# Wider product columns in the two middle token stages of an adaLN-FFN kernel, and lows moved between VectorE and GpSimd

## The reference

```python
lora_delta = lora_B @ lora_A * 0.5
wg = (weight + lora_delta).reshape(O, 16, 128)          # groups of 128 inputs
normalized = wg / exp(scale_log)
quantized = cb[searchsorted((cb[:-1] + cb[1:]) / 2, normalized)]   # 32 levels
w_eff = (quantized * scale) + lora_delta
y = x @ w_eff.T                                          # "cond"
result = y @ W_base.T + b_base                           # "ffn"
ax, probs = y @ A_w.T, softmax(y @ router_w.T)
mixed = sum over 8 experts of probs[e] * (ax @ cores[e])
out = x + result + mixed @ B_w.T * 2
```

## Time and profile before

| | |
|---|---|
| median of 3 runs | 2316.75 us (2315.3 to 2317.07) |
| profiled execution, own time | 2317.91 us |
| its span, first to last instruction | 2316.1 us |
| mean granted TensorE clock | 0.993 |
| busy: TensorE, VectorE, ACT, GpSimd | 2240.4, 1969.0, 1496.5, 1381.3 us |

### The profile page before, as it was taken

How to read it: one execution, slowest core, us unless ns; L and a number is a source line. 1 busy time by engine, 2 the same in 40 slices (tenths; PEclk the granted TensorE clock), 3 DMA queues, 4 the chain that set the end, 5 groups by cost and what they waited for, 6 DMA issues and landing times.

```text
span 2316.1 us, 31908 instructions
## 1 busy us (share of the span) xinstructions
PE 2240.4 (97%) x11610; PEld 2022.0 (87%) x11610; DVE 1969.0 (85%) x2509; ACT 1496.5 (65%) x1962; POOL 1381.3 (60%) x894
## 2 busy tenths in 40 slices
PE   3889899999999999999999999999999999999999
PEld 2445479999999989899999989899999999999998
DVE  8999998889997977999997988999996766777776
ACT  7999978989886765666664865666663664122121
POOL 6888846669874534888775635887872132333231
PEclk9999999999999999999999999999999999999999
DMA  5787855444434434666664334666656666646554
GB/s 208 261 287 274 313 211 178 163 147 156 149 129 141 116 109 177 234 239 248 246 229 156 116 105 173 226 247 253 248 211 201 186 189 186 240 190 229 194 218 155
DMA packets 133234, 459.63 MB, mean 198 GB/s; under 512 B 14114, under 2 KB 66914, under 8 KB 96354
## 3 DMA queue, kind: packets, MB, share of 16 engines
q1 hardware_dynamic: 133076, 457.59, 56.7%
HBM read 306.41 MB, written 151.13 MB: 198 GB/s over the span
## 4 chain that ended last, share of the span: by engine, by line
PE 85%; DVE 9%; ACT 3%; DMA 1%; issue 1%; POOL 0%; DVEq 0%; SPq 0%; POOLq 0%; ACTq 0%
PE m L1239 6%; PE m L1238 6%; PE m L1240 6%; DVE acc L1713 6%; PE m L1190 5%; PE m L1192 5%; PE m L1191 5%; PE m L1296 4%; PE m L1298 4%; PE m L1297 4%; PE m L1346 4%; PE m L1348 4%; PE m L1347 4%; PE m L1131 4%; PE m L1307 3%; PE m L1306 3%
## 5 line engine op out<-in xcount | busy, mean ns | idle before, releaser
L1713 DVE SCALAR_TENSOR_TENSOR acc<-mk,dj,acc 128x1024 f32<-128x1024 uint8 x736 | 943.2, 1282 | 66.3 <-ACT mk L1461 47.9
L1461 ACT ACTIVATE mk<-wr,bj 128x1024 uint8<-128x1024 f32 x736 | 811.7, 1140 | 3.0 <-DVE acc L1713 2.1
L2034 POOL TENSOR_TENSOR pp<-pp,tm 128x1024 f32<-128x1024 f32 x184 | 454.0, 2468 | 22.3 <-POOL tm L2020 0.6
L2020 POOL TENSOR_SCALAR tm<-mp,dj 128x1024 f32<-128x1024 uint8 x192 | 226.0, 1178 | 211.0 <-ACT mp L1467 203.5
L1817 DVE TENSOR_TENSOR kl<-kw,kh 128x416 fp32r<-128x416 f32 (+3 forms) x310 | 237.6, 775 | 85.8 <-ACT kh L1496 84.7
L1496 ACT ACTIVATE kh<-kw 128x416 fp32r<-128x416 f32 (+3 forms) x310 | 169.1, 548 | 182.1 <-DMA kw<-in_wb 91.8
L1239 PE MATMUL m<-gl,xh 128*128 128x384 f32 (+2 forms) x800 | 280.9, 351 | 0.0
L1238 PE MATMUL m<-gh,xh 128*128 128x384 f32 (+2 forms) x800 | 280.6, 351 | 0.0
L1240 PE MATMUL m<-gh,xl 128*128 128x384 f32 (+2 forms) x800 | 279.8, 350 | 0.0
L1467 ACT ACTIVATE mp<-wr,bj 128x1024 uint8<-128x1024 f32 x224 | 255.1, 1139 | 0.0
L1773 DVE TENSOR_TENSOR part<-m,part 128x512 f32<-128x512 f32 (+4 forms) x362 | 217.6, 610 | 30.9 <-PE m L1240 16.6
(11 more groups left out here) (249 smaller groups left out, 5169.8 us busy)
## 6 DMA issues: line engine op xcount, KB each, us to landing
part<-part SPq DMA_DIRECT2D x191, 1036.0 KB, 4.8
rows<-in_wb SPq DMA_DIRECT2D x61, 1036.0 KB, 4.8
out<-part SPq DMA_DIRECT2D x31, 1024.0 KB, 4.8
kw<-in_ws SPq DMA_DIRECT2D x128, 208.0 KB, 2.7
xw<-in_x SPq DMA_DIRECT2D x96, 256.0 KB, 3.3
kw<-in_wb SPq DMA_DIRECT2D x92, 192.0 KB, 2.4
wr<-in_w SPq DMA_DIRECT2D x32, 512.0 KB, 5.9
dl<-delta SPq DMA_DIRECT2D x30, 512.0 KB, 5.3
```

Source lines behind the costliest of these rows:

```text
L1461: e.activation(R.mk[m % NM], w, ACT.Identity, bias=R.bj[:, j:j + 1], scale=GROW).then_inc(S["mk"], 1)
L1713: e.scalar_tensor_tensor(R.acc, R.mk[m % NM], R.dj[:, j:j + 1], R.acc, ALU.mult, ALU.add).then_inc(S["ac"], 1)
L2034: e.tensor_tensor(R.pp, first, R.tm[scaled_level(q, i)], ALU.add).then_inc(S["pp"], 1)
```

## The change

Seven things change together.

1. `SW` becomes 680. A product's 680 columns are two matmuls of 340 in neighbouring banks (one PSUM tensor `mm` of five banks; a chain takes banks 0 and 1 or 2 and 3, and the chains change places from pair to pair). Rests become two pieces of 356 columns for each tile, in bank 4 and `pd`. The sums of G's blocks are 1360 wide; the fourth one doesn't fit in the wh buffers any more and lies over a quarter of G that only pair 0 reads, so it is built at pair 1.
2. Pair 15 is mixed as well; pair 1 and pair 15 have their own order of units.
3. `token_sums_low` moves from VectorE to GpSimd; the low part of a pair's second tile (`second_low`) moves from GpSimd to VectorE.
4. In W stages 1 and 2 the low part of each fourth slot (s % 4 == 3) is GpSimd's.
5. W stages 1 and 2 take three halves of levels instead of two and a half, token stages 1 and 2 five instead of five and a half; 14 units at the start and 9 at the end have no levels.
6. At the start of W stages 2 and 3 slots 2 to 5 lie in guest buffers (stage 2: x0, x1, x2 and a token sums buffer).
7. The high and low splits of the next stage's first weights take other places: highs of the last pair at units 3, 7 and 9, GpSimd's lows at 4 and 7, and in stage 1 VectorE's four lows (17, 19, 21, 23) at slots 0 to 3 of W stage 2. The tile store and the fetch of raw half 24 (`half_done`) come after the last unit that adds to the pair's first tile, in pair 15 at unit 9 of 11.

The diff, cut to its core:

```diff
-UNTIL_TOKENS, UNTIL_WEIGHTS = (16, 24, 32), (0, 18.5, 26.5, 32)
+UNTIL_TOKENS, UNTIL_WEIGHTS = (16, 24, 32), (0, 19, 27, 32)
-GUEST = {4: 2, 5: 0}
-GUEST_LAST = {2: 0, 3: 1, 10: 0, 11: 1}
+GUEST = {1: {4: "x2", 5: "x0"}, 2: {2: "x0", 3: "x1", 4: "x2", 5: "sums"},
+         3: {2: "g0", 3: "g1", 4: "x2", 5: "x0", 10: "g0", 11: "g1"}}
-SW = 512
-REST = (HX - SW) // 3 * 2
-MIX = (("prod", 1), ("prod", 2), ("rest", 0, 0), ("rest", 0, 1), ("prod", 6), ("prod", 5), ("rest", 0, 2), ("prod", 7),
-       ("prod", 3), ("rest", 1, 0), ("prod", 4), ("rest", 1, 1), ("rest", 1, 2))
+SW = 680
+SPLIT_SW, REST = 340, HX - SW
+CHAIN_AT = (512 - SPLIT_SW, 3 * 512 - SPLIT_SW)
+MIX = (("prod", 1), ("prod", 2), ("rest", 0, 0), ("prod", 6), ("prod", 5), ("rest", 0, 1), ("prod", 7), ("prod", 3),
+       ("rest", 1, 0), ("prod", 4), ("rest", 1, 1))
+MIX_START = (("prod", 1), ("prod", 2), ("rest", 0, 0), ("rest", 0, 1), ("prod", 6), ("prod", 5), ("rest", 1, 0), ("prod", 7),
+             ("prod", 3), ("rest", 1, 1), ("prod", 4))
+MIX_END = (("prod", 1), ("rest", 0, 0), ("prod", 5), ("prod", 6), ("rest", 0, 1), ("prod", 3), ("prod", 7), ("rest", 1, 0),
+           ("prod", 2), ("prod", 4), ("rest", 1, 1))
-MIX_FIRST, MIX_LAST = 1, PAIRS - 2
+MIX_FIRST, MIX_LAST = 1, PAIRS - 1
-SPREAD_AT, SPREAD_HIGH_AT = (0, 1, 3), (1, 2, 3, 4)
-SPREAD_LOW, SPREAD_LOW_AT = (2, 0, 1, 3), ((0, 4), (0, 5), (0, 6), (1, 2))
+SPREAD_AT, SPREAD_HIGH_AT = ((0, 0), (0, 2), (1, 0)), ((0, 1), (0, 3), (0, 4), (1, 1))
+SPREAD_LOW, SPREAD_LOW_AT = (0, 1, 2, 3), ((0, 5), (0, 6), (1, 1), (1, 5))
+HIGH_SPLIT_AT = {1: {3: (16, 20), 7: (18, 22, 17), 9: (19, 21, 23)}, 2: {3: (24,), 7: (26, 25, 27)}}
+LOW_SPLIT_AT = {1: {4: (16, 20), 7: (18, 22)}, 2: {4: (24,), 7: (26,), 9: (25,), 10: (27,)}}
+LOW_SPLIT_LATER = {2: (17, 19, 21, 23), 3: ()}
-WAIT_LEVELS, END_LEVELS, WAIT_SLOTS = 8, 11, 4
+WAIT_LEVELS, END_LEVELS, WAIT_SLOTS = 14, 9, 4
...
+def weight_by_pool(g, s):
+    return g < LAST and s % 4 == 3
+def unit_chain(u):
+    return (u[0] + (u[2] in (2, 3, 5))) % 2
+def low_by_vector(g, t):
+    return g in MIXED and mixed(t // 2) and t % 2 == 1
...
# mixed_tokens_of
-            if at == (11 if mixed(p) else 9) and mixed(p + 1):
+            if at == (MIX_OF[p].index(("prod", 3)) + 2 if mixed(p) else 9):
                 yield ("token_sums_high", g, p + 1)
-                if p:
-                    yield ("token_sums_low", g, p + 1)
-            if (p, at) == (1, 1):
-                yield ("token_sums_low", g, 1)
-            if (p, at) == (1, 5):
+                yield ("token_sums_low", g, p + 1)
+            if (p, at) == (0, 8):
                 yield ("late_normalised", g)
-        if at == (9 if mixed(p) else 5):
+        if p == PAIRS - 1 and at == 5:
+            yield ("next_weights", g)
+        if at == half_done_at(p):
             yield ("half_done", g, p)
-        if p == PAIRS - 1 and at == 6:
-            yield ("next_weights", g)
...
# tensor_program.mul
+            n, first = at[0], CHAIN_AT[unit_chain(UNITS_OF[g][k])]
+            pieces = ((0, SPLIT_SW), (SPLIT_SW, SW))
+                for c0, c1 in pieces:
+                    e.matmul(R.mm[:, first + c0:first + c1], high, oh[:, c0:c1], start=kp == 0 and n in (1, 2, 5), stop=False,
+                             skip_group_check=n in (3, 4, 6, 7))
+                # the same for (high, ol) and (low, oh)
...
# vector_program
+    def second_low(g, t):
+        xw, xl, xh = R.token(g, t)
+        e.wait_ge(S["xh"], NT * g + t + 1)
+        e.wait_ge(S["qs"], 4 * sums_count(g, t // 2))
+        e.tensor_tensor(xl, xw, xh.bitcast(F32), ALU.subtract).then_inc(S["xd"], 1)
...
# gpsimd_program
+    def weight(g, s):
+        w = slot_width(g, s)
+        e.wait_ge(S["gh"], NS * (g - 1) + s + 1)
+        kw, kl, kh = R.ring(g, s)
+        e.tensor_tensor(kl[:, 0:w], kw[:, 0:w], kh[:, 0:w].bitcast(F32), ALU.subtract).then_inc(S["pl"], 1)
```

More of the change, by code:

```diff
@@ L524, in first_at_home @@
 def first_at_home(g, s):
-    guests = {**GUEST, **(GUEST_LAST if g == LAST else {})}
-    return s not in guests and all(k in guests for k in range(s % RING, s, RING))
+    return s not in GUEST[g] and all(k in GUEST[g] for k in range(s % RING, s, RING))
 def wait_consumed(e, S, q):
@@ L537, in wait_consumed, with weight_lows, wait_weight @@
         e.wait_ge(S["used"], NS * g)
+def weight_by_pool(g, s):
+    return g < LAST and s % 4 == 3
+def weight_lows(g, s, pool):
+    return sum(1 for i in range(1, g + 1) for u in range(slots_of(i)) if (i, u) <= (g, s) and weight_by_pool(i, u) == pool)
+def wait_weight(e, S, g, s):
+    if weight_by_pool(g, s):
+        e.wait_ge(S["pl"], weight_lows(g, s, True))
+    else:
+        e.wait_ge(S["gl"], weight_lows(g, s, False))
 def wait_final_row(e, S, k):
@@ L556, in units_of_stage @@
         if mixed(p):
-            units += [(p, *u) for u in MIX]
+            units += [(p, *u) for u in MIX_OF[p]]
         else:
@@ L631, in sums_free, with pool_lows, vector_lows, wait_low @@
 def sums_free(g):
-    return multiplied(g, prod_unit(g, MIX_LAST, 3))
+    return multiplied(g, max(prod_unit(g, MIX_LAST, n) for n in (3, 5, 6, 7)))
+def low_by_vector(g, t):
+    return g in MIXED and mixed(t // 2) and t % 2 == 1
+def pool_lows(g, t):
+    places = [(i, u) for i in range(g + 1) for u in range(NT) if (i, u) <= (g, t)]
+    return sum(1 for i, u in places if not low_by_vector(i, u))
+def vector_lows(g, t):
+    return NMIX * (g - 1) + t // 2 - MIX_FIRST + 1
+def wait_low(e, S, g, t):
+    if low_by_vector(g, t):
+        e.wait_ge(S["xd"], vector_lows(g, t))
+    else:
+        e.wait_ge(S["xl"], pool_lows(g, t))
 def x_buffer(g, t):
@@ L2168, in gpsimd_program @@
         elif what == "slot":
+            g, s = at
             if at == (LAST, 20):
                 clear()
-        elif what == "x_split" and at[0] and at[1] < 2 or what == "x_low":
+            if s + AHEAD < slots_of(g) and weight_by_pool(g, s + AHEAD):
+                weight(g, s + AHEAD)
+        elif what == "x_split" and at[0] and at[1] < 2:
             split_x(*at)
+        elif what == "x_low":
+            if not low_by_vector(*at):
+                split_x(*at)
         elif what == "late_normalised":
```

185 lines of the change are left out of this document (104 added, 81 removed), and 2 rows, old and new, of the table COMPUTE.

## The result

After: median **2341.78 us** (2340.35 to 2344.77, 4 runs) against 2316.91 (2315.3 to 2317.57, 4 runs) of before on the same chip. The ratio is 1.0113, 95% interval 1.0098 to 1.0127. The kernel is 25 us slower; 2306 was forecast, with a range of 2300 to 2316, so the time lies outside it and on the other side.

What follows compares the result with a forecast made beforehand. TensorE's own stream was taken to bound the token stages. Less 13.6 us of stream and 4.4 of waits, more 1 + 2 + 2.9 + 1.2 = 7.1: net -10.9 from 2317.91, 2306 us as median, range 2300 to 2316.

Steps and rivals of the forecast that it cites:

- the sum's 4.4: From first middle W stage to last token stage: TensorE's 4.4 us of waits for VectorE's additions counted as gone.
- The saving: Mixed pairs in token stages: fewer columns but more matmuls save TensorE 0.36 us a pair, from 21.13 to 20.77.
- 13.6: TensorE's stream in both mixed token stages: 10.1 us less over 28 pairs plus 3.5 for pair 15 becoming mixed.
- Rival A: Token stages: 340-column matmuls cost what 348 cost, 9 us less saving, 2315; chance 0.08.
- B: Only the columns count and the waits put on GpSimd don't come: 19.9 us less, about 2298; chance 0.12.
- 2.9 was forecast: GpSimd in the token stages: its slack, waiting for VectorE's last level, goes from 5.8 to 2.9 us a half.
- D: GpSimd becomes the bound of the token stages through the sums' low part: 21 us more, 2327; chance 0.10.
- whether the three other engines still deliver: Second part of the prediction's question: whether the engines beside TensorE keep up in the shorter time.
- load per pair: VectorE in the token stages: -0.1 us a pair, so its load doesn't grow; about 96% busy, still hidden.
- about as much after: VectorE in the second middle W stage: busy 152 of 181 us, and about as much after the change.
- The 2.9 + 1.2 us that I had for W2: Second middle W stage: GpSimd's low parts late for TensorE, 2.9 us at slot 3 and 1.2 at slot 67.
- Rival C: GpSimd's low parts of W late at all eight chunk changes in both middle W stages: +8.4 us, 2314; chance 0.10.

Runs made afterwards that it cites:

- Experiment 1: Changed kernel, with the next pair's second-token partial result loaded behind both x loads on SyncE's queue instead of ahead of them: 2324.2 us, ratio to before 1.0026.
- experiment 11: Changed kernel with x loaded first, token sums' low part back on VectorE and second token's back on GpSimd: 2322.88 us, ratio to before 1.0024.
- experiment 4: Changed kernel with the token sums' low part back on VectorE and the second token's back on GpSimd, x loads unchanged: 2329.57 us, ratio to before 1.0054.
- experiment 5: Changed kernel with x loaded first and two and a half halves of levels in the middle W stages instead of three: 2328.22 us, ratio to before 1.005.
- experiment 8: Changed kernel with x loaded first, two and a half halves in the middle W stages, all low parts of W on VectorE: 2318.16 us, ratio 1.001.
- experiment 12: x loaded first, 680 columns and mixed last pair, all else as in the kernel before: 2316.95 us, ratio to before 1.0002.
- experiment 13: x first, 680 columns, mixed last pair, else as before; VectorE's levels from half 16 over 768 of 1024 columns: 2306.57 us, ratio 0.9958.
- experiment 14: Kernel before, with VectorE's level additions from half 16 on over 768 of 1024 columns: 2314.94 us, ratio to before 0.9999.
- experiment 2: Changed kernel with all low parts of W on VectorE, none on GpSimd: 2343.78 us, ratio to before 1.0116.
- Experiment 6: Changed kernel with x loaded first and the low part of slot 3 of the second middle W stage on VectorE: 2320.24 us, ratio to before 1.0013.
- experiment 16: Changed kernel with x loaded first and VectorE's level additions from half 16 on over 768 of 1024 columns: 2315.18 us, ratio to before 0.9997.
- experiment 9: Changed kernel, x first; three halves and GpSimd's W low parts in first middle W stage, two and a half and none in second: 2317.83 us, ratio 0.9999.
- experiment 10: Changed kernel, x first, GpSimd's W low parts in first middle W stage alone, two and three quarter halves in each: 2325.87 us, ratio 1.0036.

## Why the prediction was wrong

**What held.** TensorE's waits before, and that its own stream set these stages. (The prediction's text gives 2.5 us of waits to the token stages; the rows give 3.7, and with W2's 0.7 the sum's 4.4 is right. Experiment 1 has 1.1 us of such waits, 1 was forecast. There were also 2.5 us of waits for low parts in the last W stage, which the change doesn't touch.) The pair: 20.87 us against 20.77. The saving is 0.26 us a pair, not 0.36: two matmuls of 340 columns start every 0.311 to 0.316 us, one of 356 every 0.164:

```profile
1049.05 0.47 PE L1364 MATMUL m<-gh,xl 128*128 128x340 f32 x2
1049.36 0.47 PE L1358 MATMUL m<-gh,xh 128*128 128x340 f32 x2
...
1051.24 0.33 PE L1373 MATMUL m<-gh,xh 128*128 128x356 f32 x1
1051.40 0.33 PE L1374 MATMUL m<-gl,xh 128*128 128x356 f32 x1
```

Over whole units that is 155.5 and 162.8 ns. 7 x 12 x 0.1555 + 4 x 12 x 0.1628 = 20.88. The line through the earlier trace rows gives 154.8 and 162.0. Solved from the two pairs alone (21.13 us for 46,656 columns in 114 matmuls, 20.87 for 45,648 in 132), the fixed part of a matmul is 9 ns, an estimate, and above the 2 to 6 that the prediction allowed. So the term is 28 x 0.26 + 3.4 (two last pairs at 1.7) = 10.7 us, not 13.6. Rival A had 9 us less saving, 21.09 a pair; the pair came out a third of the way to it. (B's 2298 is counted from the profiled execution; from the median, as the forecast, it is 2297.)

VectorE's durations: 0.86 us for an addition of 680 columns (0.9 forecast), 1.15 to 1.36 for the second token's low part (1.3). GpSimd's sums' low part took 2.45 (2.6), and it still waited 16.1 us in three waits for VectorE's last level between 937 and 1215, 5.4 each, where 2.9 was forecast (the terms given add up to 3.1); with x first it waited 25.2 us in five, 5.0 each. TensorE waited 3.1 us in two for that low part in after and not at all in experiment 1: GpSimd never bounded the token stages, D fell (experiment 11).

**The step that failed: "whether the three other engines still deliver".** The prediction works out VectorE, by its load, and GpSimd. For the token stages the DMA queue is not worked out, and the sum puts nothing for x coming late, though the change moves the store that x stands behind: the first token's last product is now unit 8 of 11 and ends 5.8 us before the pair does instead of 7.1, and the second token's low part, moved to VectorE, stands ahead of its addition. The store goes 2.2 and 3.3 us (medians of the two stages) ahead of the next pair instead of 5.1 to 6.2. A "load per pair" that "doesn't grow" says nothing about when that one addition is done. The row that shows the slack was there to be asked: before, SyncE waited 62 us in 25 waits for TensorE ahead of its x loads in T1. That was the reserve, some 2.5 us a wait, behind the store's landing and the part load. Price: 21.9 us in the two token stages (experiment 1, profiled executions; 17.6 by the medians). TensorE's named waits there are 15.3 us in after and 1.1 in experiment 1, and about 4.5 us are the clock (below). Putting the low parts back without touching x takes 11.5 of the 21.9 away (experiment 4); what the new order of units costs alone no run shows.

**The second: the levels in the W stages, put down as hidden.** That VectorE's "load per pair doesn't grow" is true only because half a half of levels moved to the W stages, and there the prediction has VectorE "busy 152 of 181 us now" and "about as much after". It became 162 and 167, with W1 2.9 and W2 13.6 us longer. The 2.9 + 1.2 us that I had for W2 were real places, 5.3 and 1.2, but the share of busy time was the wrong reading for the rest: a slot's low part is due every 2.09 us and `gl` at every change of chunk, and each level ahead of one on VectorE is 1.28 us. With the levels back in the token stages these are VectorE's at 98 to 99% and as long as before (experiments 5, 8, 12). So even the mended change was worth nothing: the 10.7 us lie behind VectorE, and most of them come out only when it is relieved (8.4 to 9.6 us, experiments 13 and 14). That experiment 13 takes 2306.57 us, about the time forecast, is chance: it is another kernel, and leaves out a quarter of the level sums.

Rival C named GpSimd's low parts at the changes of chunk. Waits of this kind cost 5.6 us in five places, not 8.4 in eight, and taking them away moved them to VectorE (experiment 2). None of the rivals was what happened: D had the side and, with 2327, the nearest time, by a mechanism that experiment 11 rules out. A rival on SyncE's queue had no chance given.

**Why W2 loses 13 us and W1 only 3**, with the same number of levels, can be added up. In all the profiles a middle W stage takes 181.7 to 183.3 us, plus TensorE's named waits in it, plus half of the time that the clock stands at its 1.2 GHz level. After, W1 has 2.4 us of waits and no such time. W2 has 11.2 us of waits, 5.3 of them slot 3's, and 1.7 us of clock. Experiment 6 has 8.7 and 5.1, experiment 16 has 8.4 and 3.4, and experiments 4 and 11, the longest with 199.2 and 199.1, have 11.2 and 5.1.

**What stays open.** Why the clock falls behind some of these waits and not behind others, which makes 1.7 to 5.1 us of W2 in the kernels with three halves there. No version that does the whole computation is faster than the kernel before: experiments 9 and 12 tie with it, and so, within 0.1%, does experiment 8.

## What to carry to other kernels

When a unit, or an operation in an engine's queue, is moved within a period, list what each DMA queue has behind the store that it releases, and read the queue's own waits: here "queue waits for TensorE" was slack and "queue waits for a landing" the bound, and a lead of 2 to 3 us instead of 5 to 6 decided 21.9 us. Where a second engine is nearly as full as the first (97% in these pairs), ask what a shorter stream on the first leaves it: here nothing was gained until work left VectorE, and moving that work to another stage moved the wait there. An experiment on the order of a queue should first be compared with the old order, instruction by instruction: one here left the order that mattered unchanged.

## What the runs showed of the hardware

A wait of TensorE can cost more than itself. In after TensorE waited 2.5 us for VectorE's addition until 1214.5; then the granted clock was (us; PE, PEld, DVE, ACT, POOL; clock):

```profile
1214.00:1216.00 2.00, 1.51 (x7) 1.51 (x8) 2.00 (x4) 2.00 (x3) 2.00 (x2) 0.79 0.91 274
1216.00:1218.00 2.00, 2.00 (x9) 2.00 (x8) 2.00 (x4) 0.68 (x2) 1.85 (x2) 0.50 0.64 265
1218.00:1220.00 2.00, 2.00 (x13) 2.00 (x12) 2.00 (x4) 2.00 (x3) 1.77 (x2) 0.86 0.01 4
1220.00:1222.00 2.00, 2.00 (x15) 2.00 (x14) 2.00 (x4) 0.97 (x1) 1.56 (x1) 1.00 0.63 265
```

0.50 is the 1.2 GHz level. About a dozen matmuls each take 0.13 us longer from start to start: 1.5 us. After has four such places (near 1215, 1257, 1515 and 1610 us, behind waits of 2.5, 5.3, 2.2 and 2.1 us); the kernel before has none between 705 and 1790 us. In experiment 10 a wait of 2.89 us was followed by thirteen matmuls of 512 columns at 0.43 us instead of 0.23. Not every wait does it: one of 2.2 us that ended at 1359.3 in after left the clock at 1.00. A change that may add waits of this size needs a term for the clock in its sum; here it was 1.5 to 3.4 us a place.

The Trainium skill (TensorE: Matmul & The Clock Gate, "HAM oscillation — how this bites in real kernels") says that waits for data in the middle of a kernel can bring the clock down. These rows agree; the page's example has waits for DMAs, and here they were for VectorE and GpSimd, the shortest 2.1 us.
